# Attention scores of two groups issued together on two row strips of TensorE, with the order of a round changed

## What is computed

```python
q = (layernorm(x) @ Wq).reshape(b, n, 32, 16); k, v = split(ctx @ Wkv)
q, k = rope(q, pos), rope(k, pos)
w = softmax(einsum('bqhd,bkhd->bhqk', q, k) / 4)
x = x + tanh(g_xattn) * (einsum('bhqk,bkhd->bqhd', w, v) @ Wout + bout)
xf = layernorm(x); probs = softmax(xf @ gate_w.T); weights, selected = top_k(probs, 6)
x = x + tanh(g_ffn) * (shared_ffn(xf) + sum over selected of weight * expert_ffn(xf))
```

## Time and profile before

| | us |
|---|---|
| median of 3 runs | 1550.06 |
| span of the profiled execution | 1563.8 |
| TensorE busy, whole span | 1471.7 |
| VectorE busy | 725.1 |
| ScalarE busy | 495.6 |
| GpSimd busy | 678.5 |

### The profile page before, as it was taken

One profiled execution on the slowest core, in us unless ns is written; L12 is line 12 of the kernel. 1 busy time (PEld: TensorE's weight loads), 2 busy tenths in 40 slices (PEclk: granted clock), 3 DMA queues, 4 the chain that ended last, 5 costly groups with the idle time before them and its releaser, 6 DMA issues.

```text
span 1563.8 us, 31992 instructions
## 1 busy us (share of the span) xinstructions
PE 1471.7 (94%) x8922; PEld 1250.2 (80%) x8923; DVE 725.1 (46%) x1555; ACT 495.6 (32%) x982; POOL 678.5 (43%) x1135
## 2 busy tenths in 40 slices
PE   4999999999999947999999999999999999999998
PEld 2666666666666636999999999999999999899998
DVE  4578777777777642222222222222222222245556
ACT  3345444444444402222222222222222222211111
POOL 3457744435343340457242444444444220545553
PEclk8799999999999758999999999999999999999999
DMA  4022421113222235442334433444332442256664
GB/s 183 18 87 73 165 109 72 72 72 113 102 72 73 80 128 189 138 137 80 131 133 137 137 131 133 134 137 137 132 123 87 137 137 81 79 154 212 192 201 154
DMA packets 76009, 190.01 MB, mean 122 GB/s; under 512 B 10451, under 2 KB 12500, under 8 KB 73268
## 3 DMA queue, kind: packets, MB, share of 16 engines
q1 hardware_dynamic: 54260, 99.28, 19.2%
q0 software_dynamic: 21696, 90.06, 16.9%
HBM read 116.80 MB, written 72.50 MB: 121 GB/s over the span
## 4 chain that ended last, share of the span: by engine, by line
PE 75%; DVE 12%; issue 5%; POOL 3%; ACT 2%; another core or an unknown queue 1%; DMA 1%; SPq 1%; DVEq 0%; ACTq 0%; POOLq 0%
PE bank L1357 35%; PE bank L1391 19%; PE bank L616 6%; PE bank L641 4%; PE bank L1327 4%; DVE smax L888 3%; PE bank L1368 3%; PE bank L654 2%; PE bank L623 2%; DVE soft L891 1%; PE bank L671 1%; POOL w_lo L209 1%; ACT soft_t L533 1%; DVE x L936 1%
## 5 line engine op out<-in xcount | busy, mean ns | idle before, releaser
L1357 PE MATMUL bank<-w_hi,x_hi 128*128 (+1 forms) x1144 | 289.5, 334 | 1.6 <-POOL w_lo L209 1.6
L1357 PE MATMUL bank<-w_hi,x_lo 128*128 (+1 forms) x1144 | 277.8, 324 | 0.0
L1357 PE MATMUL bank<-w_lo,x_hi 128*128 (+1 forms) x1144 | 277.6, 324 | 0.0
L205 POOL CAST w_hi<-w_raw 128x352 fp32r<-128x352 f32 x144 | 62.1, 479 | 449.8 <-PE bank L1357 449.8
L1447 DVE SCALAR_TENSOR_TENSOR act<-silu,row_w,bank 128x352 f32<-128x352 f32 x111 | 64.4, 581 | 319.8 <-ACT silu L1299 305.8
L1299 ACT ACTIVATE silu<-bank 128x352 f32<-128x352 f32 x143 | 66.5, 465 | 454.9 <-PE bank L1357 421.2
L1357 PEld LDWEIGHTS bank<-w_lo,x_hi 128*128 128x128 f32 x1144 | 200.2, 188 | 0.0
L1357 PEld LDWEIGHTS bank<-w_hi,x_lo 128*128 128x128 f32 x1144 | 200.1, 188 | 0.0
L1357 PEld LDWEIGHTS bank<-w_hi,x_hi 128*128 128x128 f32 x1144 | 193.3, 189 | 1.9 <-POOL w_lo L209 1.9
L1391 PE MATMUL bank<-w_hi,a_hi 128*128 (+3 forms) x429 | 170.0, 396 | 1.2 <-DVE a_lo L1435 1.2
L1391 PE MATMUL bank<-w_hi,a_lo 128*128 (+3 forms) x429 | 169.5, 395 | 0.0
(11 more groups left out here) (184 smaller groups left out, 2376.2 us busy)
## 6 DMA issues: line engine op xcount, KB each, us to landing
xr<-expert_rows SPq DMA_DIRECT2D x111, 264.0 KB
y_rows<-y SPq DMA_DIRECT2D x111, 256.0 KB, 2.0
w_raw<-in_w POOLq DMA_DIRECT2D x18, 1408.0 KB, 7.0
w_raw<-in_w POOLq DMA_DIRECT2D x18, 512.0 KB, 8.1
x_sb<-in_x SPq DMA_DIRECT2D x16, 256.0 KB
x_res<-in_x SPq DMA_DIRECT2D x16, 256.0 KB
x_rows<-x SPq DMA_DIRECT2D x16, 256.0 KB, 3.7
x_rows<-row SPq DMA_DIRECT2D x16, 256.0 KB
```

The costliest lines, as they stand in the source:

```text
L1357: last = nc.tensor.matmul(to[:, 0:WIDTH], xx[jt][:, d, :], w[d][half][:, cols], start=(d == 0 and xx is x_hi and w is w1_hi), stop=(d == D ...
```

## The change

The scores of groups u and u+1 are issued together at even u by `score_pair`, in the order: first half of u, first half of u+1, second half of u, second half of u+1. The two groups lie on neighbouring strips of 32 rows and in different banks. The pair waits until groups up to u-1 are shifted; before, group u waited for groups up to u-2. Both groups still signal `score_mm`.

The transposes of the normalised row and their copy move from u=7 of stage TAIL to u=0 of stage PLACE, which is the next round. On TensorE the transposes of the rotated k stand ahead of `probs` in slot 5, and `rank` has a further wait for the bias step. On VectorE the statistics move from u=2 to u=3, xn from u=6 to u=7, the gate's long chain from u=5 to u=3, `residual` from u=4 to u=5 and `normalised_row` from u=6 to u=7.

```diff
--- before.py
+++ after.py
@@ -535,6 +535,12 @@
 
             def one_round(at):
                 for u in range(GROUPS):
+                    if at(PLACE) and u == 0:
+                        b = at(PLACE)[0]
+                        act.wait_ge(x2_mm, b + 1)
+                        need(act, gate_mm, b)
+                        a.activation(x2_hi[:].rearrange("p c n -> p (c n)"), bank[1][:], ACT.Copy)\
+                            .then_inc(x2_hi_done, 1)
                     if at(PROJECT) and u == 0:
                         b = at(PROJECT)[0]
                         act.wait_ge(xt_mm, b + 1)
@@ -592,12 +598,6 @@
                         need(act, v_mm, b)
                         need(act, c_lo_done, b)
                         a.activation(c_hi[:], c_raw[:], ACT.Copy).then_inc(c_hi_done, 1)
-                    if at(TAIL) and u == 7:
-                        b = at(TAIL)[0]
-                        act.wait_ge(x2_mm, b + 1)
-                        need(act, gate_mm, b)
-                        a.activation(x2_hi[:].rearrange("p c n -> p (c n)"), bank[1][:], ACT.Copy)\
-                            .then_inc(x2_hi_done, 1)
                     if at(PLACE) and u == 2:
                         b = at(PLACE)[0]
                         act.wait_ge(gneg_done, b + 1)
@@ -627,22 +627,23 @@
             pe.wait_ge(small_in, 16 * 5)
             pe.wait_ge(ones_done, 2)
 
-            def scores(at, u):
+            def score_pair(at, u):
+
                 if at(ATTEND):
                     b, j, n = at(ATTEND)
                     if u == 0:
                         pe.wait_ge(qt_done, b + 1)
                         pe.wait_ge(kt_done, 2 * (b + 1))
-
-                    r = 32 * (u % 4)
-                    need(pe, shifted, b * GROUPS + u - 1)
+                    need(pe, shifted, b * GROUPS + u)
                     for c in range(2):
-                        ch = 2 * (u // 4) + c
-                        last = nc.tensor.matmul(bank[2 + u % 2][:, c * 2 * P:(c + 1) * 2 * P],
-                                                q_t[j][r:r + 32, ch, :],
-                                                k_t[j][r:r + 32, ch].rearrange("p e n -> p (e n)"),
-                                                start=True, stop=True)
-                    last.then_inc(score_mm, 1)
+                        for w in (u, u + 1):
+                            r, ch = 32 * (w % 4), 2 * (w // 4) + c
+                            last = nc.tensor.matmul(bank[2 + w % 2][:, c * 2 * P:(c + 1) * 2 * P],
+                                                    q_t[j][r:r + 32, ch, :],
+                                                    k_t[j][r:r + 32, ch].rearrange("p e n -> p (e n)"),
+                                                    start=True, stop=True)
+                            if c == 1:
+                                last.then_inc(score_mm, 1)
 
             def probs(at, u):
                 of, v = earlier(at, u, 1)
@@ -738,8 +739,10 @@
                                             start=False, stop=(c == DC - 1))
                 last.then_inc(gate_mm, 1)
 
-            def rank(b):
-
+            def rank(b, tail_at):
+
+                if tail_at:
+                    pe.wait_ge(chain_tail, TAIL_STEPS * tail_at[0] + 5)
                 pe.wait_ge(mask_done, b + 1)
                 need(pe, seen_done, b)
                 need(pe, slot_done, b)
@@ -757,7 +760,10 @@
                 for u in range(GROUPS):
                     if at(TAIL) and u == 3:
                         transpose_values(*at(TAIL))
-                    scores(at, u)
+                    if u % 2 == 0:
+                        score_pair(at, u)
+                    if at(PLACE) and u == 0:
+                        transpose_row(*at(PLACE))
                     if at(PROJECT) and u == 7:
                         project_late(u, *at(PROJECT))
                     if u in (1, 2, 3):
@@ -766,20 +772,17 @@
                         tail(u, *at(TAIL))
                     if at(PROJECT):
                         project(u, *at(PROJECT))
+                    if at(PROJECT) and u == 5:
+                        project_late(u, *at(PROJECT))
                     if u not in (1, 2, 3):
                         probs(at, u)
-                    if at(TAIL):
-                        if u == 0:
-                            tail(u, *at(TAIL))
-                        if u == 7:
-                            transpose_row(*at(TAIL))
+                    if at(TAIL) and u == 0:
+                        tail(u, *at(TAIL))
                     if at(PLACE) and u == 1:
                         gate_logits(*at(PLACE))
-                    if at(PROJECT) and u == 5:
-                        project_late(u, *at(PROJECT))
                     values(at, u)
                     if at(PLACE) and u == 6:
-                        rank(at(PLACE)[0])
+                        rank(at(PLACE)[0], at(TAIL))
                     if at(TAIL) and u == 3:
                         project_out(*at(TAIL))
                     if at(PLACE) and u == 7 and isinstance(at(PLACE)[0], int) and at(PLACE)[0] == BATCHES - 1:
@@ -850,21 +853,21 @@
                     last.then_inc(done, 1)
 
             def load(u, b, j, n):
-                if u == 2:
+                if u == 3:
                     dve.wait_ge(x_in[j], 16 * (n + 1))
                     v.bn_stats(stats[:], x_sb[j][:]).then_inc(stats1_done, 1)
                     waits_apart(dve, passed_v, (stats1_done, b + 1), (xn_done, b))
                     v.bn_aggr(mean1[:], stats[:]).then_inc(var1, 1)
                 if u == 7:
-                    dve.wait_ge(c_hi_done, b + 1)
-                    need(dve, v_mm, b)
-                    v.tensor_tensor(c_lo[:], c_raw[:], c_hi[:].bitcast(F32), ALU.subtract).then_inc(c_lo_done, 1)
-                if u == 6:
                     dve.wait_ge(var1, b + 1)
                     dve.wait_ge(rstd1_done, b + 1)
                     need(dve, xt_mm, b)
                     v.tensor_scalar(xn[:], x_sb[j][:], mean1[:, 0:1], rstd1[:, 0:1], ALU.subtract, ALU.mult)\
                         .then_inc(xn_done, 1)
+                if u == 7:
+                    dve.wait_ge(c_hi_done, b + 1)
+                    need(dve, v_mm, b)
+                    v.tensor_tensor(c_lo[:], c_raw[:], c_hi[:].bitcast(F32), ALU.subtract).then_inc(c_lo_done, 1)
 
             def project(u, b, j, n):
                 if u == 0:
@@ -957,7 +960,7 @@
                     ch.step(v.tensor_reduce(gmax[:], logits[:], AX.X, ALU.max))
                     ch.sync()
                     v.tensor_scalar(gneg[:], gmax[:], -1.0, None, ALU.mult).then_inc(gneg_done, 1)
-                if u == 5:
+                if u == 3:
                     dve.wait_ge(gexp_done, b + 1)
                     ch.step(v.reciprocal(grec[:], gsum[:]))
                     ch.sync()
@@ -1052,9 +1055,9 @@
                         tail(u, *at(TAIL), ch)
                     if at(ATTEND):
                         attend(u, *at(ATTEND))
-                    if at(TAIL) and u == 4:
+                    if at(TAIL) and u == 5:
                         residual(*at(TAIL), ch)
-                    if at(TAIL) and u == 6:
+                    if at(TAIL) and u == 7:
                         normalised_row(*at(TAIL))
                     if at(TAIL) and u == 2:
                         tail(u, *at(TAIL), ch)
@@ -1062,7 +1065,7 @@
                         project(u, *at(PROJECT))
                     if at(TAIL) and u == 0:
                         tail(u, *at(TAIL), ch)
-                    if at(PLACE) and u in (0, 1, 5):
+                    if at(PLACE) and u in (0, 1, 3):
                         gate(u, *at(PLACE), gate_ch)
                     if at(PLACE) and u == 6:
                         place(*at(PLACE))
```

## The result

The changed kernel takes 1562.12 us (median of 11 runs, 1558.72 to 1570.19) where the kernel before takes 1550.38 (11 runs). The ratio is 1.0065, with a 95% interval of 1.004 to 1.009: slower by a little, where 1528 was forecast. The page of the changed kernel's profiled execution shows the span, TensorE's busy tenths and the granted clock in tenths.

What follows compares the result with a forecast made beforehand. TensorE was taken as the bound, busy 29.52 of 31.84 us a round. Full rounds -28, partial rounds -10 and clock +16 make -22: from 1563.8 to 1541.8 us profiled, 1528 as the median, range 1500 to 1564.

Steps and rivals of the forecast that it cites:

- The pair: Phase A scores: two groups' matmuls overlap nearly wholly, 1.08 us a pair, saving 4.2 us of TensorE a round.
- rival 3: Scores: strips don't overlap, each pair takes up to 2.1 us, 30 us on the forecast, 1558 us; chance 0.10.
- The round by hand: Phase A's full round, traced by instruction: 29.5 us instead of 31.84, so 2.35 of 4.2 us saved reach it.
- Rival 4: Phase A rounds: TensorE stays the bound, stalls no larger than now, 27.6 us a round, 1484 us; chance 0.09.
- The residual and the normalised row at no cost: VectorE steps moved to u=5 and u=7: they cost nothing, the residual filling idle time before attend 6.
- The clock: Phase A rounds: lower clock in about eight of twelve, 3 us each, 24 us against some 8 now: 16 more.
- rival 2: Clock falls every round before k's transposes, for some 10 us, leaving TensorE as idle as before; 1564 us; chance 0.13.
- The rounds with parts missing: Two attention rounds ahead of the twelve full ones and two behind: 2.5 us saved each, 10 us in all.
- The difference carried over to the median: Whole kernel: profiled span 13.7 us above the median, taken over, so 1541.8 profiled becomes 1528 as the median.
- The rules of the Trainium skill: Scores: packing gives 1.06 us a pair; tiling doesn't speed PSUM evacuation, so VectorE's chain sets the round, a small gain.

Runs made afterwards that it cites:

- same_strip: The changed kernel with the pair's matmuls in the order u, u, u+1, u+1, two on one strip and then two on the next: 1561.82 us.
- qt_early: The changed kernel with ScalarE's copy of q_t one slot earlier, ahead of the exponential of group 4: 1507.75 us.
- order_qt: The changed kernel with scores issued group by group as before, and ScalarE's copy of q_t one slot earlier: 1578.91 us.
- pair_only: The kernel before with only its scores issued in pairs by score_pair, all other orders as before: 1542.07 us.

## Why the prediction was wrong, point by point

- *The pair* was put at 1.08 us. It is 1.07 (372.29 to 373.36). Right; rival 3 is out. same_strip shows that even the order within the pair is free.
- *The round by hand* was 29.5 us. It is 29.59. The stall ahead of k's transposes was put at 2.7 us and is 2.64, and the wait for exponential 0 at 0.7 and is 0.91 (358.61). The wait of 0.74 for the gate's exponential shrank to 0.26 (367.29), and one of 0.63 for at_lo (369.33) stands behind it, which the steps give only by their times. The sum of the waits is right, the parts in part by luck. VectorE has no gap from at_lo (368.58) to group 4's subtraction (374.96), as the steps said. Rival 4 is out.
- *The residual and the normalised row at no cost*: no wait of TensorE for the row shows in the round without a fall. Right.
- *The clock* is the step that failed: a term of the sum that was mis-sized. The mechanism was named; I took eight of twelve rounds at 3 us, 24 us. In the profile nine of eleven have a fall, at 33.6 against 29.6, which is 4.0 us each, 36 us. The source of the price was misread, too: the round of 35.3 us in the earlier trace rows holds ScalarE's stall, with 1.9 us of TensorE's idle time, and two low stretches of 3.4 us, of which the first comes ahead of that idle time. A low stretch of 3.4 us by itself costs 0 to 0.8 us there. What the changed kernel has is another size: stretches of 10.2 us, which cost 3.4 to 4.2, and of 13.7 us, which cost 4.9. The discount from 3.5 to 3, on the ground that VectorE is the later one anyway, was wrong as well. The low stretch of 10.2 us covers k's transposes, the pair (6,7) and the projection of v, all of them on TensorE's path: 9.86 us busy of 10.20. It was rival 2, given 0.13, that came true. That its 1564 us is so close to 1562 is in part luck: it has falls in twelve rounds at 5 us and savings of 38 us, where the profile has nine of eleven at 4.0, and it adds its 14 us to a profile which the changed kernel's undercuts by 5. Nor is TensorE idle in the low stretch, as that rival had it.
- *The rounds with parts missing*: 5 us were expected of the early two. They gave 1: x1 of round 4 starts at 116.44 against 117.43. The clock isn't the reason, since it is low for 27.3 us ahead of that in both; what took the rest isn't shown. Of the late ones 5 us were expected too, and the stretch from x1 of round 15 to phase B gave 10.1; it has 30.7 us at the low clock in the last three intervals before and 23.9 after.
- *The difference carried over to the median* was the second failed step. The span of the profiled execution of the kernel before was 13.7 us above the median of the first three runs. I took that as an offset of profiling and carried it over; in the eleven experiments the profiled span lies between 4.2 below and 7.4 us above the median, so it is no such offset. That execution has the two rounds with ScalarE's stall, 3.5 us longer than the others each, and the 10.1 us behind round 15. I booked some 8 us as the kernel's own falls and let the change replace them. That its median execution is without the stalls is a guess from its shorter time, since there is only this one profile of the kernel before. The prediction of the trace's own time, 1541.8, missed 1558.5 by 17 us; that of the median, 1528, missed 1562 by 34.
- *The rules of the Trainium skill*. TensorEngine Tiling (Array Packing), PSUM Bottleneck, has it that tiling doesn't speed up PSUM's evacuation. The undisturbed round agrees in part: VectorE is busy for 24.00 of 29.59 us, TensorE for 24.89, so neither is full, and 1.4 us of the round hung on where one copy on ScalarE stands (qt_early). The rule of the Trainium skill in TensorE: Matmul & The Clock Gate, part 3 (packing small matmuls), on tiles of different row groups agrees with 1.07 us a pair.

## What to carry to other kernels

Where TensorE is nearly full, shortening its work buys idle or thin stretches, and these can cost the clock. Look at where the saved time will gather, and let the price of a low stretch of the clock stand in the sum for every round in which it can recur. A fall is cheap to test for: put matmuls on constants into the longest stall, and if the kernel gets faster, move what ends the stall, here a copy on ScalarE by one slot. When the profiled execution is far above its median, look for long rounds in it, and for what stands still in them, before taking the difference as an offset or a price from such a round.

## What the runs showed that I had not expected

- Adding two matmuls (1.98 us) to each round made the kernel 38 us faster (1562.1 to 1523.7).
- The clock fell to 0.50 behind 8.00 us in which TensorE was busy for 8.00 us (order_qt), and didn't fall for 330 us in a kernel that idles more than the changed one (pair_only, from 157 to 487 us).
- A fall in the changed kernel lasts 10.2 or 13.7 us, three to four times the falls of 3.4 us in the middle of the kernel before, although TensorE is busy for 9.86 of the 10.20 us. Why it lasts is open.
- Matmuls on two strips run side by side even when each strip's two are issued one after the other (1.07 us a pair in either order).
